# An adaLN transformer pair: order of loads, first offsets, bias pair and third group at the head of layer 0

## The chip, the cores and the metric

The kernel runs on one core of a Trainium2 chip, as one program. The metric is the device time of one execution in microseconds; lower is better. Three executions of the kernel before are given, and one more was taken with a profile.

## The reference

Two adaLN layers over x of shape (4, 1024, 128), float32. The whole change lies in the attention of layer 0:

```python
mod = (_silu(L0_c) @ L0_wmod).reshape(L0_c.shape[0], 6, 1, -1)
sa, ca, ga, sb, cb, gb = (mod[:, i] for i in range(6))
ga = (2 * (ga >= 0) - 1) * jnp.maximum(jnp.abs(ga), 0.25)
h = _layernorm(x) * (1 + ca) + sa
# attention: linear, with a rotary-like product
qkvu = h @ Wqkvu.T + bqkvu              # q, k, v, u; 16 heads of 8
q, k = silu(q), silu(k)
q, k = [t * cos(theta * n), t * sin(theta * n)] for t in (q, k)
out = einsum(q, k) @ v                  # no softmax, so q (k^T v)
out = u * layernorm(out, ln_w, ln_b)
x = x + ga * (out @ Wout.T + bout)
# then: layernorm, modulation, top-2 routing to 8 experts with capacity,
# and a second layer (cosformer attention, 16 routed experts)
```

## The kernel before

Layer 0 works in eight groups of four token tiles (a group is 512 tokens, `G4 = 4`, `NGRP = 8`); two groups are one batch. All engines have a hand-written program each, and they meet only at semaphores. An engine works strictly in the order of its list, so the order of the calls is the schedule.

**Loads.** `l0_sync` (line 188 on) issues all loads from SyncE's queue, one behind the other: the first quarter of the first batch's x (line 196), theta (197), `consts` (198: identity, masks, ones, 713 columns), modulation's weights `wmod` (199, 768 columns), the early rows with the bias of keys and values (200), layer 0's projection weights (201), the second quarter of x (202), then the rest. ScalarE's queue loads `cols`, the per-partition columns.

**Head of each engine's list.** VectorE (`l0_vector`, line 952) takes mean and variance of group 0 (`keys_stats(0)`, helper `variances`, lines 797 to 802), builds the rotation angles for half of the positions (`angles_vector(0)`, lines 760 to 769), takes the statistics of group 1, builds the bias pair (line 790, the key bias split in a high and a low part), closes the angles (lines 776 to 784), builds the other half, and then rotates keys (line 818) and queries (line 845) as they come. `keys_stats(2)` stands behind the first query rotation. GpSimd (`l0_gpsimd`) turns variances into inverse roots and offsets: `keys_roots(u)` gives the negated mean (line 233), the root (line 228) and their product (line 236), the offset that ScalarE adds. It then makes the gate columns (lines 243 to 249), the gated bias `gbo` (line 259), the gated output weights (line 267), and later it sends each tile's rows to the experts' buffer with two indirect DMAs a tile (line 291).

ScalarE (`l0_scalar`) normalises a group (`keys_normed`, line 622: scale and offset), evicts the transposed group with the modulation on it (`keys_modulated`, line 631), makes silu of the keys (line 638), keeps the values (line 644), u and the queries (lines 659, 662), the angles' sines (lines 605, 607) and the transposed rotation tables (`rotation_kept`, line 613). TensorE (`l0_tensor`) makes the modulation (`mod_tensor`, line 348), transposes a group (`keys_turned`, line 385), projects keys (lines 395, 399) and values (line 408), adds up the state k^T v over a batch (`keys_state`, line 436), projects u (line 416) and q (line 422), and multiplies the rotated queries with the state (`outputs_tensor`, line 448).

**The loop.** When groups 0 and 1 have given the first state, a loop over g from 0 to 5 handles output group g, key group g + 2 and input group g - 1 together. In it ScalarE squares the outputs (line 668) for their variance, VectorE gates them (`outputs_gated`, line 854), rotates keys g + 2 (line 818), reads the variances (line 860), rotates the queries of g + 1 (line 845), adds to x (lines 869, 876, 885), takes statistics (line 797) and routes (lines 905 to 950). The input's transposes, bias matmuls and rows are lines 491, 469 and 504 of TensorE. `S["l0_root1"]` counts three increments for each unit of `keys_roots`.

After layer 0's last dispatch the experts' matmuls start from the dispatched rows, and layer 1 follows.

Of the kernel before, what the change touches and what calls it, by code (L numbers as in the profile page):

```python
# [75 lines left out]
class Kernel:  # L76
# [113 lines left out]
    def l0_sync(self):  # L190
        sp, S, io = self.sp, self.S, self.io
# [4 lines left out]
        sp.dma_start(X(0)[:, 0:G4, :], x(0)[:, 0:G4, :]).then_inc(S["dma_x0"], 16)  # L196
        sp.dma_start(self.rowsb[:, 0:D], row(0, D)).then_inc(S["dma_cols"], 16)
        sp.dma_start(self.consts[:], io["consts"]).then_inc(S["dma_consts"], 16)
        sp.dma_start(self.wmod[0][:], io["wmod0"]).then_inc(S["dma_wmod0"], 16)
        sp.dma_start(self.rowsb[:, D:early], row(D, early)).then_inc(S["dma_rows"], 16)  # L200
# [28 lines left out]

    def keys_roots(self, u):  # L230
        g, S, at = self.pool, self.S, self.UNITS[u]
        g.wait_ge(S["ln1"], u + 1)
        g.tensor_scalar(self.nm1[:, at], self.mv1[:, at, 0], -1.0, None, ALU.mult).then_inc(S["l0_root1"], 1)
        self.inverse_root(self.y1[:, at], self.t1[:, at]).then_inc(S["l0_root1"], 1)
        g.wait_ge(S["l0_root1"], 3 * u + 2)
        g.tensor_tensor(self.nm1[:, at], self.nm1[:, at], self.y1[:, at], ALU.mult).then_inc(S["l0_root1"], 1)
# [115 lines left out]
    def gate_tensor(self, lay):  # L352

        pe, S, bank = self.pe, self.S, self.bank
        pe.wait_ge(S["mod_wide"], lay + 1)
        pe.wait_ge(S["dma_consts"], 16)
        if lay:
            pe.wait_ge(S["l0_x"], NGRP)
        for j in range(2):
            for b in range(B):  # L360
                ins = pe.matmul(bank[6 + j][:, b * D:(b + 1) * D], self.gateB[:, j, b, :], self.c["ident"], start=True,
                                stop=True)
            ins.then_inc(S["mod_B"], 1)
# [15 lines left out]
    def keys_turned(self, a):  # L379
        pe, S, bank = self.pe, self.S, self.bank  # L380
        pe.wait_ge(S["l0_xn"], a + 1)
        pe.wait_ge(S["l0_hT"], a)
        pe.wait_ge(S["l0_h2T"], max(0, a - 3))
        for i in range(G4):
            ins = pe.transpose(bank[0][:, i * P:(i + 1) * P], self.xn[:, i, :], self.c["ident"])
# [136 lines left out]
    def l0_tensor(self):  # L522
# [16 lines left out]
        for g in range(NGRP - 2):  # L539
            a, c = g + 2, g - 1  # L540
            self.keys_turned(a)
            self.outputs_tensor(g)
            self.keys_projected(a)
            self.values_projected(a)
# [151 lines left out]
    def l0_scalar(self):  # L696
# [19 lines left out]
        self.rotation_sines(1)  # L716
        self.queries_kept(1)
        self.rotation_kept(1)
        self.keys_normed(2)
        for g in range(NGRP - 2):  # L720
            a, c = g + 2, g - 1
            self.keys_modulated(a)
            self.outputs_squared(g)
            self.keys_silu(a)
            if c >= 0:
# [27 lines left out]
    def angles_vector(self, half):  # L753
# [9 lines left out]
        v.wait_ge(vs.sem, k)  # L763
        k = vs.did(v.tensor_scalar(cnt[:], th[:], 1.0 / TWO_PI, ROUND, ALU.mult, ALU.add))
        v.wait_ge(vs.sem, k)
        k = vs.did(v.tensor_scalar(cnt[:], cnt[:], ROUND, None, ALU.subtract))
# [37 lines left out]
    def keys_stats(self, u):  # L804
# [3 lines left out]
        tiles = [self.X[:, n, :] for n in range(at.start, at.stop)]  # L808
        self.variances(tiles, self.kst1[:, 0:len(tiles), :], self.mv1[:, at, :], self.t1[:, at]).then_inc(S["ln1"], 1)

    def keys_rotated(self, a):
# [140 lines left out]
    def l0_vector(self):  # L952
        v = self.dve
        v.memset(self.label[:], 0.0)
        self.keys_stats(0)
        self.angles_vector(0)
        self.keys_stats(1)
        self.bias_pair()
        self.angles_closed(0)
        self.angles_vector(1)  # L960
        self.keys_rotated(0)
        self.angles_closed(1)
        self.queries_rotated(0)
        self.keys_stats(2)
        self.keys_rotated(1)
# [1664 lines left out]
```

## Time and profile before

| | |
|---|---|
| three executions | 876.41, 876.96, 877.82 us; median 876.96 |
| profiled execution, its own time | 876.81 us |
| its span, first to last instruction | 875.5 us |
| TensorE matmul busy | 813.9 us (93%) |
| VectorE busy | 610.6 us (70%) |
| ScalarE busy | 434.1 us (50%) |
| GpSimd busy | 399.7 us (46%) |
| mean granted clock of TensorE | 0.969 of full |

The span is what the views of the trace cover; the execution's own time is 1.3 us longer. Busy times overlap, so they don't add up to the span. Matmuls are pipelined, so TensorE's busy share is not its share of peak. The chain of waits is followed back from the last instruction to what released each step.

### The profile page before, as it was taken

Reading aid. Unit: us, or ns where it says so; the run is one execution under the profiler, and the core shown is the slowest. Engines: PE = TensorE matmul, PEld = TensorE weight load, DVE = VectorE, ACT = ScalarE, POOL = GpSimd, SP = SyncE. Lnnn points to the kernel's source line nnn. Section 1 sums busy time; section 2 is a strip of 40 time slices with the busy share of each in tenths; the row PEclk is TensorE's granted clock in tenths of the full one; section 3 lists DMA queues with packets and bytes.
Section 4 is the critical chain, followed back from the end, with each engine's and each line's share of the span. In section 5 each row is a group of like instructions: output and inputs, shape, how many; then the busy total and the mean of one; then the engine's idle time right before and its main releaser. Section 6 shows DMA issues by size and latency. Waiting matters only on the chain.

```text
span 875.5 us, 32569 instructions
## 1 busy us (share of the span) xinstructions
PE 813.9 (93%) x13678; PEld 702.7 (80%) x13678; DVE 610.6 (70%) x1760; ACT 434.1 (50%) x947; POOL 399.7 (46%) x404
## 2 busy tenths in 40 slices
PE   6999985399997799999999999999999999999998
PEld 5777755389996688888888888888888888878887
DVE  7788894475663676675677685786866777758875
ACT  5556532443443756555556465464564564433222
POOL 5348887324454554644545654456442342410000
PEclk9999995599998999999999999999999999999999
DMA  9714100434232100000100100200000000027761
GB/s 297 246 52 169 35 29 11 130 121 119 84 93 72 45 27 4 28 3 3 50 4 3 29 3 3 53 3 3 4 3 3 5 3 3 4 52 147 153 134 40
DMA packets 67904, 49.66 MB, mean 57 GB/s; under 512 B 5297, under 2 KB 62784, under 8 KB 67376
## 3 DMA queue, kind: packets, MB, share of 16 engines
q1 hardware_dynamic: 64288, 42.41, 18.0%
q0 software_dynamic: 3328, 5.16, 1.8%
q8 instruction: 109, 1.79, 0.9%
q14 instruction: 35, 0.29, 0.1%
q10 hardware_dynamic: 144, 0.02, 0.0%
HBM read 33.20 MB, written 16.10 MB: 56 GB/s over the span
## 4 chain that ended last, share of the span: by engine, by line
PE 76%; DVE 7%; issue 6%; POOL 5%; ACT 3%; DMA 1%; SPq 0%; ACTq 0%; POOLq 0%; DVEq 0%
PE psum L1477 11%; PE psum L1580 8%; PE psum L1607 7%; PE psum L1558 7%; PE psum L1165 6%; PE psum L2224 5%; PE psum L1510 5%; PE psum L1539 5%; PE psum L2242 4%; PE psum L1595 3%; PE psum L1521 3%; POOL disp L291 3%; PE psum L1495 3%; PE psum L1200 3%; POOL sb_l_y L228 1%
## 5 line engine op out<-in xcount | busy, mean ns | idle before, releaser
L2122 POOL TENSOR_TENSOR sb_a_qr<-sb_h,sb_a_csq 128x512 f32<-128x512 f32 x64 | 81.5, 1296 | 113.8 <-PE psum L1580 107.9
L2122 POOL TENSOR_TENSOR sb_a_qr<-sb_a_qp,sb_a_csq 128x512 f32<-128x512 f32 (+1 forms) x64 | 72.3, 1152 | 116.8 <-PE psum L1580 116.8
L1477 PE MATMUL psum<-sb_wkv,sb_a_hs 128*128 128x512 f32 x384 | 122.2, 427 | 1.9 <-DVE sb_a_hs L1931 1.6
L1734 ACT ACTIVATE sb_a_vr<-sb_a_va,sb_consts 128x520 f32<-128x520 f32 x128 | 86.6, 727 | 5.1 <-DVE sb_a_va L1982 4.7
L291 POOL DMA_INDIRECT disp<-sb_h,sb_slot x64 | 68.7, 1073 | 25.9 <-issue 16.1
L1477 PEld LDWEIGHTS psum<-sb_wkv,sb_a_hs 128*128 128x128 f32 x384 | 63.8, 191 | 13.6 <-DVE sb_a_hs L1931 2.0
L1580 PE MATMUL psum<-sb_a_vr,sb_a_kb 64*64 64x130 f32 x1920 | 73.0, 277 | 1.9 <-issue 1.9
L2003 DVE TENSOR_TENSOR sb_a_mid<-psum,sb_a_state 128x130 f32<-128x130 f32 x112 | 47.4, 424 | 36.6 <-PE psum L1580 36.5
L1111 POOL DMA_INDIRECT chosen<-sb_m_h3t,sb_e_row x40 | 39.4, 985 | 69.3 <-ACTq L1279 53.7
L1558 PE MATMUL psum<-sb_a_mid,sb_a_qr 64*64 64x65 f32 x2048 | 70.6, 218 | 0.0
L1165 PE MATMUL psum<-sb_e_xt,sb_e_ws 128*128 128x320 f32 x384 | 63.8, 321 | 4.5 <-DVE sb_e_hs L1359 3.7
L1711 ACT ACTIVATE sb_h<-psum,sb_cols 128x512 f32<-128x512 f32 x32 | 22.0, 688 | 90.8 <-PE psum L1510 90.8
L1607 PE MATMUL psum<-sb_a_wo,sb_a_ot 128*128 128x128 f32 x512 | 65.5, 281 | 0.0
L1580 PEld LDWEIGHTS psum<-sb_a_vr,sb_a_kb 64*64 64x64 f32 x1920 | 56.9, 132 | 10.3 <-issue 4.9
L1558 PEld LDWEIGHTS psum<-sb_a_mid,sb_a_qr 64*64 64x64 f32 x2048 | 65.1, 134 | 0.0
L1165 PEld LDWEIGHTS psum<-sb_e_xt,sb_e_ws 128*128 128x128 f32 x384 | 58.1, 193 | 8.2 <-issue 5.1
L1558 PE MATMUL psum<-sb_a_state,sb_a_qr 64*64 64x65 f32 x1792 | 62.8, 218 | 0.0
L2224 PE MATMUL psum<-sb_m_hs,sb_wgus 128*128 128x512 f32 x240 | 60.9, 401 | 0.7 <-DVE sb_m_hs L2357 0.7
L1607 PEld LDWEIGHTS psum<-sb_a_wo,sb_a_ot 128*128 128x128 f32 x512 | 59.6, 192 | 1.7
L2300 ACT ACTIVATE sb_m_sg<-psum 128x512 f32<-128x512 f32 x40 | 23.9, 599 | 70.9 <-PE psum L2224 70.9
L1558 PEld LDWEIGHTS psum<-sb_a_state,sb_a_qr 64*64 64x64 f32 x1792 | 58.0, 134 | 0.0
L1982 DVE TENSOR_TENSOR sb_a_va<-psum,sb_rows 128x512 f32<-128x512 f32 x64 | 44.0, 688 | 15.8 <-PE psum L1477 15.8
(276 smaller groups left out, 1946.8 us busy)
## 6 DMA issues: line engine op xcount, KB each, us to landing
sb_h<-turned SPq DMA_DIRECT2D x32, 256.0 KB, 5.5
sb_e_w<-in_w SPq DMA_DIRECT2D x24, 256.0 KB, 3.2
chosen<-sb_empty SPq DMA_DIRECT2D x8, 512.0 KB, 6.5
sb_a_g<-chosen SPq DMA_DIRECT2D x12, 256.0 KB, 3.5
disp<-sb_empty SPq DMA_DIRECT2D x4, 650.0 KB, 9.8
sb_e_x<-disp SPq DMA_DIRECT2D x7, 325.0 KB, 5.2
sb_a_wo<-in_wo SPq DMA_DIRECT2D x4, 512.0 KB, 5.2
out<-sb_x SPq DMA_DIRECT2D x7, 256.0 KB, 3.9
```

Of the source, the lines that this page charges most:

```text
L291: g.indirect_dma_start(out=self.disp, out_offset=bass.IndirectOffsetOnAxis(ap=self.slot[:, k, n:n + 1], axis=0), in_=self.H2[:, n, :], in_ ...
L1165: ins = pe.matmul(bank[2 * (n % 2) + w][:, 0:HC], self.ews[:, i, wp, w, m * P:(m + 1) * P], self.xeT[:, i, xp, cols], start=(k == 0), stop ...
L1477: ins = pe.matmul(self.values_bank(i) if kv else self.bank[0], hs[:, part, at:at + P], self.Wkv[ws][:, h, w], start=(k == 0), stop=(k == 2))
L1510: ins = pe.matmul(self.bank[2], self.Wq[ws][:, j // PH, (j % PH) * P:(j % PH + 1) * P], hs[:, part, :], start=(k == 0), stop=(k == 2))
L1558: ins = pe.matmul(self.bank[4 + q][c * DH:(c + 1) * DH, j * 65:(j + 1) * 65], Qr[p, k, j, r * DH:(r + 1) * DH], states[r][p, j, k, :], sta ...
L1580: ins = pe.matmul(self.bank[bk][q * DH:(q + 1) * DH, at:at + 130], Kb[t, 2 * j + q, :], Vr[t, 2 * j + q, :, :].rearrange("p k d -> p (k d) ...
L1607: ins = pe.matmul(self.bank[1][:, 0:D], self.oT1[:, m, :], self.Wog[b % 2][:, m, :], start=(m == 0), stop=(m == HD // P - 1))
L1734: ins = act.activation(self.Vr[i % 2][:, :, k, :], self.Va[i % 3][:], ACT.Copy, scale=self.c[("cos1", "sin1")[k]][:, n:n + 1])
L1982: v.tensor_tensor(self.Va[i % 3][:, :, 0:DH], self.values_bank(i).rearrange("p (h d) -> p h d", d=DH), self.c["bv1"][:, h * 512:(h + 1) * ...
L2003: ins = v.tensor_tensor(part(mid), first, part(state), ALU.add)
L2122: ins = g.tensor_tensor(self.Qr[i % 2][:, k, :, t], qp, rows(self.csQ[:, k, c * P + t.start:(c + 1) * P], PH), ALU.mult)
L2224: ins = pe.matmul(self.hidden_bank(t, w), self.Wgus[wp][:, w, blk * P:(blk + 1) * P], hs[:, xp, :], start=(n == 0), stop=(n == 2))
```

## The change

It exchanges two loads on SyncE's queue, moves TensorE's wait for the constants from the gate matmuls to the first transpose, gives the first group's offsets to VectorE (one instruction, -mean times root, put into `angles_vector(0)` before its third group of instructions; GpSimd keeps the root alone), puts VectorE's bias pair ahead of the second statistics and its third statistics ahead of the first query rotation, lets ScalarE normalise the third group before it copies the second half of the rotation tables, and in the loop's first turn puts TensorE's key projection before the outputs and ScalarE's silu of the keys before the square.

```diff
         sp.dma_start(self.rowsb[:, 0:D], row(0, D)).then_inc(S["dma_cols"], 16)
+        sp.dma_start(self.wmod[0][:], io["wmod0"]).then_inc(S["dma_wmod0"], 16)
         sp.dma_start(self.consts[:], io["consts"]).then_inc(S["dma_consts"], 16)
-        sp.dma_start(self.wmod[0][:], io["wmod0"]).then_inc(S["dma_wmod0"], 16)
...
     def keys_roots(self, u):
+
         g, S, at = self.pool, self.S, self.UNITS[u]
         g.wait_ge(S["ln1"], u + 1)
+        if u == 0:
+            self.inverse_root(self.y1[:, at], self.t1[:, at]).then_inc(S["l0_root1"], 1)
+            return
...
         pe.wait_ge(S["mod_wide"], lay + 1)
-        pe.wait_ge(S["dma_consts"], 16)
...
         pe.wait_ge(S["l0_h2T"], max(0, a - 3))
+        if a == 0:
+            pe.wait_ge(S["dma_consts"], 16)
...
             self.keys_turned(a)
-            self.outputs_tensor(g)
-            self.keys_projected(a)
+            if g == 0:
+                self.keys_projected(a)
+                self.outputs_tensor(g)
+            else:
+                self.outputs_tensor(g)
+                self.keys_projected(a)
...
         self.queries_kept(1)
+        self.keys_normed(2)
         self.rotation_kept(1)
-        self.keys_normed(2)
         for g in range(NGRP - 2):
             a, c = g + 2, g - 1
             self.keys_modulated(a)
-            self.outputs_squared(g)
-            self.keys_silu(a)
+            if g == 0:
+                self.keys_silu(a)
+                self.outputs_squared(g)
+            else:
+                self.outputs_squared(g)
+                self.keys_silu(a)
...
         k = vs.did(v.tensor_scalar(cnt[:], th[:], 1.0 / TWO_PI, ROUND, ALU.mult, ALU.add))
+        if half == 0:
+            self.first_keys_offsets()
         v.wait_ge(vs.sem, k)
...
+    def first_keys_offsets(self):
+        v, S, at = self.dve, self.S, self.UNITS[0]
+        v.wait_ge(S["l0_root1"], 1)
+        v.scalar_tensor_tensor(self.nm1[:, at], self.mv1[:, at, 0], -1.0, self.y1[:, at], ALU.mult, ALU.mult
+                               ).then_inc(S["l0_root1"], 2)
...
         self.angles_vector(0)
+        self.bias_pair()
         self.keys_stats(1)
-        self.bias_pair()
         self.angles_closed(0)
         self.angles_vector(1)
         self.keys_rotated(0)
         self.angles_closed(1)
+        self.keys_stats(2)
         self.queries_rotated(0)
-        self.keys_stats(2)
         self.keys_rotated(1)
```

## Rows read from the trace of the kernel before

**Rows 1.** Chain of waits: start us, us, what
```profile
34.29 1.10 PE psum L399 x8
...
60.90 1.22 POOL disp L291
```

**Rows 2.** Windows: us, busy (x instructions) by engine, PEclk, DMA share, GB/s
```profile
51.00:52.00 1.00, 1.00 (x7) 1.00 (x7) 0.55 (x1) 0.85 (x2) 1.00 (x3) 0.50 0.00 0
...
60.00:80.00 20.00, 19.30 (x132) 15.22 (x131) 16.56 (x69) 11.94 (x24) 15.79 (x14) 1.00 0.64 225
```

**Rows 3.** VectorE's timeline: start, us, line, tiles, [idle before <-releaser]
```profile
6.58 0.43 DVE L766 TENSOR_SCALAR sb_cnt<-sb_cnt 128x512 f32<-128x512 f32 x1
...
10.00 0.87 DVE L797 BATCH_NORM_STATS2 sb_l_st<-sb_x 128x6 f32<-128x128 f32 x4 [0.79 <-DMA sb_x<-in_x]
...
11.40 0.33 DVE L790 SCALAR_TENSOR_TENSOR sb_l_pair<-sb_l_high,sb_cols,sb_rows 2x128 fp32r<-2x128 f32 x1
...
13.79 0.69 DVE L784 SCALAR_TENSOR_TENSOR sb_tokt<-sb_tokt 128x512 f32<-128x512 f32 x1
...
18.68 2.40 DVE L818 TENSOR_TENSOR sb_kr<-sb_ks,sb_tokt 128x512 f32<-128x512 f32 x2
...
23.71 1.29 DVE L845 TENSOR_TENSOR sb_qr<-sb_q_t,sb_dimt 128x512 f32<-128x512 f32 x2
24.91 0.87 DVE L797 BATCH_NORM_STATS2 sb_l_st<-sb_x 128x6 f32<-128x128 f32 x4
...
36.04 1.30 DVE L818 TENSOR_TENSOR sb_kr<-sb_ks,sb_tokt 128x512 f32<-128x512 f32 x2 [0.77 <-ACT sb_ks L638]
```

**Rows 4.** GpSimd's timeline
```profile
5.48 0.30 POOL L233 TENSOR_SCALAR sb_l_nm<-sb_l_mv 128x4 f32<-128x4 f32 x1 [3.54 <-DVE sb_l_t L802]
5.75 1.30 POOL L228 TENSOR_TENSOR sb_l_y<-sb_l_t,sb_cols 128x4 f32<-128x4 f32 x1
7.12 0.67 POOL L236 TENSOR_TENSOR sb_l_nm<-sb_l_nm,sb_l_y 128x4 f32<-128x4 f32 x1
...
12.75 1.44 POOL L228 TENSOR_TENSOR sb_l_y<-sb_l_t,sb_cols 128x4 f32<-128x4 f32 x1
...
26.49 0.62 POOL L233 TENSOR_SCALAR sb_l_nm<-sb_l_mv 128x4 f32<-128x4 f32 x1 [5.96 <-DVE sb_l_t L802]
...
28.61 0.20 POOL L236 TENSOR_TENSOR sb_l_nm<-sb_l_nm,sb_l_y 128x4 f32<-128x4 f32 x1
```

**Rows 5.** ScalarE's timeline
```profile
27.73 1.06 ACT L613 COPY sb_dimt<-psum 128x512 f32<-128x512 f32 x2
28.84 1.65 ACT L622 ACTIVATE sb_xn<-sb_x,sb_l_nm,sb_l_y 128x128 f32<-128x128 f32 x4
31.24 0.78 ACT L631 ACTIVATE sb_h_t<-psum,sb_mt 128x512 f32<-128x512 f32 x1 [0.75 <-PE psum L385]
```

**Rows 6.** SyncE's queue: start and length of the issue of the constants
```profile
1.78 0.42 SPq L198 DMA_DIRECT2D sb_consts<-in_consts  x1
```

**Rows 7.** DMA issues: count, KB each, median us from issue to landing
```profile
sb_consts<-in_consts SPq DMA_DIRECT2D x1, 356.5 KB, 5.0
```

**Rows 8.** TensorE's timeline
```profile
7.81 2.73 PE L348 MATMUL psum<-sb_sc,sb_wmod 128*128 128x4 f32 x12 [7.81 <-DMA sb_wmod<-in_wmod]
...
27.81 1.96 PE L436 MATMUL psum<-sb_v,sb_kr 128*128 128x129 f32 x16
...
31.90 1.96 PE L448 MATMUL psum<-sb_qr,sb_kvc 128*128 128x512 f32 x4 [0.70 <-issue]
```

**Rows 9.** Chain of waits in two turns of the loop, at half and full clock
```profile
50.20 0.91 PE psum L491 x4
...
52.82 1.52 PE psum L504 x8
...
65.67 0.66 PE psum L491 x4
...
67.21 1.18 PE psum L504 x8
```

## The prediction, made before the changed kernel ran

> **What bounds the kernel now.** I read the chain of waits first, then the windows by stage, then each engine's timeline from 0 to 60 us. In the chain the third group's key projection holds 34.29 to 35.39 us, and the first dispatch of tokens to the experts' buffer is at 60.90 [rows 1]; the experts start behind the last dispatch. Whatever reaches the first dispatch earlier can pass to the end, because from there GpSimd is the paced engine: 15.79 of 20 us busy from 60 to 80 us, the rest being the gaps between its dispatches [rows 2]. So the question is how much earlier VectorE starts the third group's key rotation, its 36.04 us row [rows 3]; behind that row its timeline runs without a gap into the statistics that release GpSimd's next roots.
>
> In the front itself VectorE sets the pace: it waits 0.79 us for the second quarter of x, starts at 10.00, and its rows then follow each other without idle time up to the statistics of the third group at 24.91 [rows 3]. Those release GpSimd's three root instructions at 26.49, which end at 28.61 + 0.20 = 28.81 [rows 4]; ScalarE normalises at 28.84 and modulates at 31.24 [rows 5].
>
> **The change, part by part.**
> 1. *wmod before constants.* Same two issues, same bytes behind them; only their places at 1.78 us and the next slot are exchanged. The constants landed 5.0 us after issue, at 6.8 [rows 6, 7]; wmod was waited for until 7.81 [rows 8]. I take wmod at 6.9 and constants at 7.75 (their sizes differ by a tenth). TensorE starts its modulation 0.9 earlier. Constants are wanted by ScalarE's bias copies, by GpSimd's copies and now by the first transpose; all come after 7.75, so nothing is queued for long behind the moved wait.
> 2. *First offsets by VectorE.* GpSimd dropped two instructions: 0.30 before the root, 0.67 behind it. The root (1.30) now starts at 5.48 and ends at 6.78 [rows 4]. VectorE stops ahead of its second count instruction, which started at 6.58 [rows 3], until 6.82, adds one small instruction, and goes on about 0.35 later. The nearest row to that instruction is the bias pair, the same operation on 128 columns: 0.33, with the next one starting 0.26 behind it [rows 3]. On 4 columns I take 0.1; bounds 0 and 0.26, so the delay is 0.25 to 0.5. Cover: the 0.79 wait for x. Without that cover it would cost 0.35. Normalising starts near 7.0 in place of 7.83.
> 3. *Bias pair before the second statistics.* It took the path from 11.40 to 11.66 [rows 3]. Now it needs ScalarE's high part: normalising from 7.0, 1.65 long as at 28.84 [rows 5], then two short copies, about 9.1. VectorE arrives at 10.00 - 0.79 + 0.35 = 9.55, finishes by 9.85, inside the same wait for x. Gain on the VectorE path **0.26**; if ScalarE is late by over 0.8, the gain goes.
> 4. *Results for ScalarE and GpSimd at the head.* First modulated tile, gate columns, second normalising are all about 0.9 earlier. Nothing of this ends on the path: the angles on VectorE gate the first key rotation. Only ScalarE's query step of the second group gains: between 0 and 0.9, I take 0.35, as TensorE's unchanged projections stand between. The gate-times-bias product on GpSimd (128x512) comes 0.9 earlier too. In the trace the first rotation took 2.40 against 1.29 for the same shape in the query rotation [rows 3], 1.1 of it beside that product. I leave the 1.1 unchanged: the product now meets the last angle instruction and then the rotation; bounds 0 (all of it hidden, gain 1.1) and a second blocked instruction (loss 0.7).
> 5. *Third statistics before the first query rotation.* Query rotation started at 23.71, statistics at 24.91: 1.20 sooner, plus the 0.26. GpSimd starts at 26.49 - 1.46 = 25.03. Its three instructions took 2.32 (26.49 to 28.81). Now they run wholly beside VectorE's two-input instructions. At 7.12, beside VectorE's angle instructions, the last of the three took 0.67, not 0.20 [rows 4], so 2.32 to 2.8: offsets ready at 27.35 to 27.8, I take **27.7** against 28.81. The query rotation moves by its own length to 24.9 and the second key rotation still ends at its old time less 0.26, as the order changes but not the sum.
> 6. *ScalarE normalises before copying the rotation.* The copies started 27.73 and took 1.06; the normalising was at 28.84 and took 1.65 [rows 5]. ScalarE is free at about 27.4, so: normalise 27.7 to 29.35, copies to 30.35, modulate (0.78) to 31.1; before, 31.24 + 0.78 = 32.02. TensorE's state matmuls end at 27.81 + 1.96 - 0.22 = 29.55 [rows 8], the transposes follow at once, ready by 30.2, before ScalarE wants them.
> 7. *Key projection before outputs, silu before square.* Projection (1.1 for its last matmuls [rows 1]) ends at about 32.3, silu at 33.0; before, silu came behind the outputs. Outputs started at 31.90 [rows 8], directly behind the second state. That comes 0.22 sooner, but they now wait for the projection: 32.2, which costs **+0.3**. Its square and the gated product move with it; the product ended at 36.04 - 0.77 = 35.27, now at 35.55. The keys are ready by then, so the 0.77 that VectorE waited for them [rows 3] is gone. Key rotation starts at 35.5 in place of 36.04.
>
> **Sum.** -0.77 (wait for keys) + 0.3 (outputs behind projection), so **-0.47 us** at 36.04, and with step 5 at its short end (27.35, projection 0.2 sooner) about -0.65. All that follows (variance, roots of group 3 and 4, statistics) is released by VectorE or by GpSimd behind VectorE; the variance matmuls had been done before VectorE came to them. I carry the middle, -0.55, to the end. The profiled execution took 876.81 (span 875.5), 0.15 under the median of the runs, 876.96; taking the median: 876.96 - 0.55 = **876.4**.
>
> **A rule that speaks against it.** In the trace a root (12.75, 1.44) had VectorE's angle instruction, both inputs in SBUF, start inside it at 13.79 and take its usual 0.69 [rows 3, 4]: a small GpSimd instruction did not hold VectorE off. The Trainium skill, "SBUF — State Buffer", Who interferes with whom, says that of a VectorE instruction with two SBUF inputs and a GpSimd instruction that reads SBUF the later one is blocked until the first is through. By that rule the third root, now placed among two rotations, would stop VectorE for up to its 1.44, and the time would lie between the forecast and rival C; the 2.40 row agrees with the rule, the 0.69 row [rows 3] does not.
>
> **Rivals.**
> - *A, less than it says.* wmod lands no sooner (both transfers share the same engines), or the sum is lost at another engine, for example ScalarE's copies holding the modulation. Without step 1, ScalarE is free at 27.75, modulation at 31.2 becomes 31.4, and -0.55 shrinks to -0.3: **876.7**. For: the two landings lie only 1 us apart. Against: the constants did land a full microsecond sooner than wmod.
> - *B, the clock.* TensorE's granted clock is half (1.2 GHz) from 51 to 52 us [rows 2], behind short gaps in its work. That iteration's matmuls up to the routing ended 52.82 + 1.52 = 54.34, counted from the transposes at 50.20 that is 4.14; one iteration later at the full 2.4 GHz the same stretch is 65.67 to 68.40, 2.73 (its last piece 1.18) [rows 9]. It is on the path. If the changed timing spares it, another 1.4: 876.4 - 1.4 = **875.0**. For: only a short fall, so little may avoid it. Against: the gaps stay.
> - *C, slower: GpSimd holds VectorE.* If each of the three instructions of step 5 gets in front of a rotation and keeps it off, VectorE loses 0.25 + 1.45 + 0.20 = 1.9 between 25 and 29 us. The second key rotation, the state and the outputs go with it: outputs at 33.5 to 35.4, key rotation of group three at 36.75, 0.7 later than before: **877.7**. It decides once over 1.2 us of blocking falls before the second key rotation ends. Against: the 13.79 row [rows 3].
> - *D, the clock the other way.* A further half-clock stretch on the path, the same 1.4 [rows 9] on top: **877.8**. TensorE has fewer gaps from 29 to 36 than before, which speaks against.
>
> **How the numbers follow.** 0.2% is 1.75 us, about what a measurement of this kernel can tell from no change. The forecast, 876.4, has 0.58; A 0.12, B 0.20, C 0.05, D 0.05. Faster by over 0.2% is under 875.2: most of B and a small part of the forecast (product of step 4 wholly hidden, -1.1 more): 0.24. Slower is over 878.7: C or D with another loss on top, 0.05. Same 0.71. The range takes in B and the small ends of C and D: 874.8 to 877.7.
>
> **What the changed profile would show.** wmod's matmuls near 6.9; normalising of the first group near 7.0; no bias pair between the second statistics (still 10.0) and the angles; angles 0.26 sooner; GpSimd's third root from 25.0; normalising 27.7; outputs' matmuls 32.2, behind the projection; key rotation at 35.5 without a wait for ScalarE's keys; first dispatch at 60.3; last dispatch landing 0.55 sooner. Wrong if: x's second quarter lands later than 10.0; VectorE stands longer at the first offsets than 0.79; the second key rotation takes over 1.3; or the first dispatch moves and the end does not.

## The result and the profile after

| | median of the kernel before | median after | ratio, 95% interval |
|---|---|---|---|
| eight executions each, one chip | 877.32 us | **874.40 us** | 0.9967 [0.9957, 0.9977] |

The change makes the kernel 2.9 us (0.33%) faster; the interval leaves out both the forecast of 0.55 us and no change. The forecast of 876.4 us and its whole range, 874.8 to 877.7, missed the median. The profiled execution took 874.18 us (span 872.9), against 876.81 (875.5).

Landmarks in the two profiles, in us from the start of the span. Start of VectorE's rows unless another engine is named:

| | before | after | difference |
|---|---|---|---|
| second statistics (x's second quarter has landed) | 10.00 | 10.34 | +0.34 |
| third statistics | 24.91 | 23.75 | -1.16 |
| ScalarE's third normalising | 28.84 | 27.77 | -1.07 |
| TensorE's first outputs | 31.90 | 32.09 | +0.19 |
| key rotation of group 3 | 36.04 | 35.30 | -0.74 |
| TensorE's first input transposes | 50.20 | 49.46 | -0.74 |
| first dispatch on GpSimd | 60.90 | 58.75 | -2.15 |
| span | 875.5 | 872.9 | -2.6 |

Two things stand out. The key rotation came 0.74 sooner although x had landed 0.34 later, so the part in between became **1.08 us** shorter: twice the forecast. And between transposes and first dispatch another 1.41 us went. A last 0.45 of the span's 2.6 went behind the first dispatch; it was not traced.

VectorE's timeline after (start, us, line, tiles, idle before and its releaser), the rows that answer to [rows 3]:

```profile
6.74 0.16 DVE L829 SCALAR_TENSOR_TENSOR sb_l_nm<-sb_l_mv,sb_l_y 128x4 f32<-128x4 f32 x1 [0.16 <-POOL sb_l_y L228]
...
9.57 0.34 DVE L805 SCALAR_TENSOR_TENSOR sb_l_pair<-sb_l_high,sb_cols,sb_rows 2x128 fp32r<-2x128 f32 x1
10.34 0.87 DVE L812 BATCH_NORM_STATS2 sb_l_st<-sb_x 128x6 f32<-128x128 f32 x4 [0.42 <-DMA sb_x<-in_x]
...
18.84 2.27 DVE L839 TENSOR_TENSOR sb_kr<-sb_ks,sb_tokt 128x512 f32<-128x512 f32 x2
...
34.70 0.69 DVE L875 TENSOR_TENSOR sb_ou<-psum,sb_u_t 128x512 f32<-128x512 f32 x1 [1.44 <-ACT sb_sq L677]
35.30 1.28 DVE L839 TENSOR_TENSOR sb_kr<-sb_ks,sb_tokt 128x512 f32<-128x512 f32 x2
```

The first offsets wait 0.16 for GpSimd's root and take 0.16; the bias pair lies wholly inside what was a 0.79 wait for x and is now 0.42. The first key rotation still takes 2.27. VectorE no longer waits for the keys ahead of the last row; its wait is now 1.44 for the square, ahead of gating the outputs.

ScalarE's timeline after, answering to [rows 5]:

```profile
6.94 1.65 ACT L631 ACTIVATE sb_xn<-sb_x,sb_l_nm,sb_l_y 128x128 f32<-128x128 f32 x4 [1.61 <-DVE sb_l_nm L829]
...
18.92 0.69 ACT L668 ACTIVATE sb_u_t<-psum,sb_cols 128x512 f32<-128x512 f32 x1 [0.27 <-PE psum L421]
...
27.77 1.65 ACT L631 ACTIVATE sb_xn<-sb_x,sb_l_nm,sb_l_y 128x128 f32<-128x128 f32 x4
29.32 1.04 ACT L622 COPY sb_dimt<-psum 128x512 f32<-128x512 f32 x2
30.27 0.78 ACT L640 ACTIVATE sb_h_t<-psum,sb_mt 128x512 f32<-128x512 f32 x1
```

GpSimd's, answering to [rows 4]: the first root alone, the wait for the later constants, and the third group's offsets.

```profile
5.50 1.13 POOL L228 TENSOR_TENSOR sb_l_y<-sb_l_t,sb_cols 128x4 f32<-128x4 f32 x1 [3.55 <-DVE sb_l_t L817]
7.78 0.29 POOL L309 COPY sb_h<-sb_consts 128x32 f32<-128x32 f32 x1 [1.15 <-DMA sb_consts<-in_consts]
...
27.44 0.29 POOL L240 TENSOR_TENSOR sb_l_nm<-sb_l_nm,sb_l_y 128x4 f32<-128x4 f32 x1
```

TensorE's, answering to [rows 8] and the full- and half-clock rows of [rows 9]: modulation, the gate matmuls (L364), outputs, input transposes and rows.

```profile
6.80 2.51 PE L352 MATMUL psum<-sb_sc,sb_wmod 128*128 128x4 f32 x11 [6.80 <-DMA sb_wmod<-in_wmod]
...
14.93 3.09 PE L364 MATMUL psum<-sb_consts,sb_gateb 128*128 128x128 f32 x16
...
32.09 1.88 PE L453 MATMUL psum<-sb_qr,sb_kvc 128*128 128x512 f32 x4
...
49.46 0.66 PE L496 MATMUL psum<-sb_consts,sb_xn 128*128 128x128 f32 x4 [0.81 <-ACT sb_xn L684]
...
50.98 1.19 PE L509 MATMUL psum<-sb_consts,sb_h_t 128*128 128x136 f32 x8
```

The chain of waits after: from the square on it is VectorE's again, and the first dispatch stands at its end. It answers to [rows 1].

```profile
31.10 1.16 PE psum L404 x8
32.26 1.73 PE psum L453 x4
34.01 0.61 ACT sb_sq L677
...
58.75 1.22 POOL disp L295
```

The windows after, against the half clock in [rows 2]:

```profile
50.00:51.00 1.00, 1.00 (x11) 0.83 (x9) 0.81 (x2) 0.85 (x2) 1.00 (x3) 1.00 0.00 0
51.00:52.00 1.00, 1.00 (x9) 1.00 (x9) 0.69 (x1) 1.00 (x4) 1.00 (x1) 1.00 0.00 0
```

The granted clock is 1.00 (2.4 GHz) where the profile of before had 0.50 (1.2 GHz). From the transposes to the router's scores on VectorE it was 4.17 us before and is 2.75 after: that is the 1.41. So the change seems to have done rival B on top of twice the forecast. The experiments show that only the latter is the change's.

### The profile page after: what moved, and what is told of

It is laid out like the page before. It is cut to its first block, busy times and chain, and to the rows that moved or that the text cites. A ratio compares the mean times of both kernels' runs of the same rounds, so it can differ in the third digit from the quotient of the medians.

```text
span 872.9 us, 32569 instructions
## 1 busy us (share of the span) xinstructions
PE 813.6 (93%) x13678; PEld 702.2 (80%) x13678; DVE 610.7 (70%) x1761; ACT 433.8 (50%) x947; POOL 397.8 (46%) x402
## 4 chain that ended last, share of the span: by engine, by line
PE 76%; DVE 7%; issue 6%; POOL 5%; ACT 3%; DMA 1%; SPq 0%; ACTq 0%; POOLq 0%; DVEq 0%
PE psum L1498 11%; PE psum L1601 8%; PE psum L1628 7%; PE psum L1579 7%; PE psum L1186 6%; PE psum L2245 5%; PE psum L1531 5%; PE psum L1560 5%; PE psum L2263 4%; PE psum L1542 3%; PE psum L1616 3%; POOL disp L295 3%; PE psum L1516 3%; PE psum L1221 3%; POOL sb_l_y L228 1%
```

## The experiments

I write **S** for the stretch from the second statistics to group 3's key rotation (26.04 before, 24.96 after). It takes out when x lands. The chips of the experiments take about 10 us longer for either kernel; part of it lies behind the head (in the whole change's profiles the experts' part, up to layer 1's first projection, took 118 to 122 us for 114). All times are medians, compared with the kernel before on the same chip; 12 or 11 executions each unless one is named.

**The parts, and a filler for the clock.** The third group alone:

```diff
+        self.keys_normed(2)
         self.rotation_kept(1)
-        self.keys_normed(2)
...
+        self.keys_stats(2)
         self.queries_rotated(0)
-        self.keys_stats(2)
```

and with it keys_projected(a) and keys_silu(a) first in the turn g == 0, as in the change.

> Only the third group's part: third statistics before the first query rotation, normalising before the rotation copies, and in the loop's first turn keys before outputs. Theory T1 (the order of the third group makes the shift, and the half-clock stretch at 50.7 us of the profiled run of before goes by chance of its phase): key rotation of group 3 at 35.7 against 36.04 (the bias pair's 0.26 is not saved), first dispatch 0.35 us sooner where the half-clock stretch is still there and 1.75 sooner where not; median 0.5 to 2 us under before. Theory T2 (the half-clock stretch goes because TensorE's work from 29 to 47 us lies otherwise; it is this part that moves it): the stretch is gone in nearly all runs, so about 1.8 to 2.2 us under before. Theory T3 (the head, not the third group, carries the gain): under 0.3 us.

Measured: 888.34 us against 889.60, ratio 0.9995 [0.9977, 1.0012]; S 25.59.

The head alone: exchanged loads, moved wait, first offsets, bias pair; the rest as before.

> Only the head: wmod before the constants, first offsets by VectorE, bias pair before the second statistics. T1: 0.2 to 0.3 us sooner at the key rotation of group 3 (the bias pair's 0.26), the half-clock stretch as often as in before: median 0.2 to 0.6 under before. T2: half-clock stretch stays, 0.25 under before. T3: more than half of the 2.9 us of the whole change.

Measured: 888.73, ratio 0.9990 [0.9969, 1.0010]; S 25.71.

The kernel before with eight idle matmuls into an unused bank, so that TensorE's gaps ahead of the input transposes are filled:

```diff
             self.squares_summed(g)
+            if g == 1:
+                pe, bank = self.pe, self.bank
+                pe.wait_ge(self.S["l0_x"], 1)
+                for i in range(2):
+                    pe.matmul(bank[7][:, 0:P], self.c["ident"], self.c["ident"], start=True, stop=True)
             self.normed_output(g)
+            if g == 1:
+                for i in range(6):
+                    pe.matmul(bank[7][:, 0:P], self.c["ident"], self.c["ident"], start=True, stop=True)
             if g:
                 self.input_turned(c)
```

> The kernel before with 8 matmuls more, in the gaps of TensorE at 47.9 and 49.4 us, into a PSUM bank that is free there; they are no part of the computation. If the half-clock stretch at 50.7 comes from these gaps and lies on the path: no half clock between 50 and 55, the stretch from the input's transposes to the routing 2.8 in place of 4.1, the kernel about 1.4 us under before (1.0 to 1.6, where the fillers hold the transposes up by up to 0.2). If the stretch is rare in runs of before: no difference. If its cause lies earlier: it stays.

Measured: 889.96, ratio 1.0011 [0.9994, 1.0029]; full clock at the transposes (2.71 us from them to the scores), S 26.04. The transposes themselves stood 0.36 later behind the second statistics (40.56 for 40.20), so the scores came 1.10 sooner. The whole change with the same filler:

> The whole change with the same 8 matmuls. T1 and T2: the half-clock stretch is already gone in most runs, so the same as the changed kernel within 0.4 us, 2.4 to 3.2 under before. If phases decide (T1) and some runs of the changed kernel still have it, a little faster than the changed kernel.

Measured: 887.73, ratio 0.9989 [0.9974, 1.0004]; S 24.96.

What follows: the parts gave -0.45 and -0.33 of S, the whole -1.08, so 0.30 came only with both. The table further down shows where: in the third group alone ScalarE started the normalising 0.34 behind its offsets. The filler brought the full clock in its profile and no time in the median, which would have had to fall by about 1.1 us if the kernel before usually had the half clock there; the interval allows 0.5.

**The unchanged kernel again, and the whole, on a second chip**, with two that leave a part out of the whole. Leaving out the third group's sooner norm:

```diff
+        self.rotation_kept(1)
         self.keys_normed(2)
-        self.rotation_kept(1)
...
+        self.queries_rotated(0)
         self.keys_stats(2)
-        self.queries_rotated(0)
```

Leaving out the sooner keys:

```diff
-            if g == 0:
-                self.keys_projected(a)
-                self.outputs_tensor(g)
-            else:
-                self.outputs_tensor(g)
-                self.keys_projected(a)
+            self.outputs_tensor(g)
+            self.keys_projected(a)
...
-            if g == 0:
-                self.keys_silu(a)
-                self.outputs_squared(g)
-            else:
-                self.outputs_squared(g)
-                self.keys_silu(a)
+            self.outputs_squared(g)
+            self.keys_silu(a)
```

> The kernel before, run as if it were a changed one: what difference two equal programs show on this chip, and whether the half-clock stretch at 50 us is there in another of its profiles. All theories: no difference, ratio within 0.1% of 1. T1 (the stretch is a matter of phase): it may be absent at 50 us. T2 (it is a fixture of the old order): it is there.

> The whole change again, in the same batch. Counted from the start of the second statistics (the landing of x's second quarter) its third key rotation comes 1.08 us sooner than in before, as in the first pair of profiles. T1: the runs' medians differ by 1.0 to 1.6 us, and the 2.9 of the first comparison is not reached again unless this chip's runs of before spend more windows at half clock. T2: 2.5 to 3 us.

> The whole change without the third statistics and the third normalising moved ahead; the loop's first turn still has keys before outputs. T1: the modulated third group comes no earlier than in before less 0.26, so keys first holds the outputs back until about 33.2, and the key rotation of group 3, counted from the second statistics, is later than with the whole change by 1.0 or more: no gain left or a loss to 0.3 against before. Rival (keys first pays by itself): it keeps over half of the 1.08.

> The whole change with outputs before keys in the first turn, as before. T1: the outputs start with the state, 0.26 to 0.33 sooner, but keys and silu stay behind them, so the key rotation of group 3 gains those 0.3 only: 25.7 us behind the second statistics, against 26.04 in before and 24.96 with the whole change. Rival (the early normalising pays by itself): 25.3 or less.

Measured: unchanged 889.22 (ratio 0.9982 [0.9956, 1.0008], which shows how much of 0.2% chance leaves); whole 887.79, 0.9972 [0.9946, 0.9998]; no sooner norm 889.18 and no sooner keys 889.25, one execution each.

The whole's windows here:

```profile
49.00:50.00 1.00, 0.94 (x5) 0.94 (x6) 1.00 (x3) 0.48 (x2) 1.00 (x1) 0.50 0.00 0
50.00:51.00 1.00, 1.00 (x6) 1.00 (x6) 0.41 (x1) 0.79 (x2) 1.00 (x3) 0.50 0.00 0
```

The half clock at the transposes (49.06 here) is back with the whole change, S being 24.95, and it is absent from the unchanged kernel's profile. In all 20 profiles it falls on this place in 6: the kernel before's first, the whole's here and in a later run, and those of three other versions. The mean granted clock of the timed executions agrees: in the three later comparisons of the whole it was 0.969 for both, over 35 executions of the whole and 85 of the kernel before. **Whether the half clock falls there is chance in either kernel; the 1.41 us of the first pair is not the change's.**

S was 25.71 without the sooner keys, just the head's, although the third normalising stood 1.11 us sooner than in the head (17.43 us behind the second statistics for 18.54). So in the old order the normalising doesn't set S. The chain of waits of this version passes through the second state and VectorE's closing of it (`sb_kvc`) to the outputs:

```profile
28.11 2.07 PE psum L440 x16
...
31.78 0.44 DVE sb_kvc L847
32.22 0.09 issue
32.31 1.96 PE psum L452 x4
```

The sooner norm needs the sooner keys to count. Without the sooner norm S was 27.66, but with the half clock at the outputs (33 to 36 us; 3.52 us for them, 1.96 in [rows 8]), so I took it again below.

The unchanged kernel gave the surprise: **S 27.04 in place of 26.04**. Its TensorE, ScalarE and second key rotation:

```profile
16.65 3.08 PE L361 MATMUL psum<-sb_consts,sb_gateb 128*128 128x128 f32 x16
...
20.63 0.69 ACT L659 ACTIVATE sb_u_t<-psum,sb_cols 128x512 f32<-128x512 f32 x1 [0.28 <-PE psum L416]
...
27.06 1.29 DVE L818 TENSOR_TENSOR sb_kr<-sb_ks,sb_tokt 128x512 f32<-128x512 f32 x2
...
28.51 1.04 PE L376 MATMUL psum<-sb_consts,sb_tokt 128*128 128x128 f32 x8
...
29.38 1.96 PE L436 MATMUL psum<-sb_v,sb_kr 128*128 128x129 f32 x16
...
30.23 1.65 ACT L622 ACTIVATE sb_xn<-sb_x,sb_l_nm,sb_l_y 128x128 f32<-128x128 f32 x4
```

against the first profile of the same kernel:

```profile
16.08 2.08 PE L361 MATMUL psum<-sb_consts,sb_gateb 128*128 128x128 f32 x16
...
19.16 0.69 ACT L659 ACTIVATE sb_u_t<-psum,sb_cols 128x512 f32<-128x512 f32 x1
...
26.34 1.30 DVE L818 TENSOR_TENSOR sb_kr<-sb_ks,sb_tokt 128x512 f32<-128x512 f32 x2
...
26.94 1.04 PE L376 MATMUL psum<-sb_consts,sb_tokt 128*128 128x128 f32 x8
...
31.38 0.42 DVE L835 SCALAR_TENSOR_TENSOR sb_kvc<-sb_kvs,sb_kvm 128x256 f32<-128x256 f32 x1
```

TensorE's first matmuls take about twice as long as the same ones later (L399 x8 2.08 at 12.51 us, 1.16 once the group comes round again), until some point between 15 and 19 us. The clock column prints 1.00 there in every profile, so I go by durations; "the clock rises" in the expectations means this point. Here it fell behind the 16 gate matmuls, which took 3.08. ScalarE waited for them and its u came 1.47 later. So did what follows in TensorE's and ScalarE's lists: the transposes of the second half of the rotation tables (L376) and, 0.87 behind them, the second state (L436), 1.57 later than in the first profile, though its key rotation was through at 28.35; and the third normalising, 1.4 later and long after its offsets (ready at 28.92). x itself had landed 0.57 later.

**Once more, for the spread.** Whole and unchanged again, no sooner norm again, and a version of the whole in which VectorE rotates group 3's keys before it gates the first outputs, in the idle time in front of the square:

```diff
-            self.outputs_gated(g)
-            if c >= 0:
+            if g == 0:
+                self.keys_rotated(a)
+                self.outputs_gated(g)
+            else:
+                self.outputs_gated(g)
                 self.input_means(c)
-            self.keys_rotated(a)
+                self.keys_rotated(a)
```

> The whole change a third time. Key rotation of group 3 starts 24.96 us behind the second statistics (before: 26.04). If the shift of 1.08 us is all that the change does beside chance in the clock's windows, the means over all batches come to 1.0 to 1.4 us under before; if the change also spares half-clock windows as a rule, its runs show about one window fewer each than those of before and a mean of 1.8 to 2.5 us under.

> The kernel before once more as a partner: its mean number of half-clock windows and its time should fall with the runs of before, within 0.1%. It tells how large a difference comes from nothing.

> The whole change without the earlier third statistics and normalising, again, as in the last look a half-clock window fell on its output matmuls (3.52 us for 1.96). At full clock its key rotation of group 3 starts 26.1 us behind the second statistics: keys first gives nothing without the earlier normalising. If 25.7 or less, the two parts are independent.

> The whole change, and VectorE in the loop's first turn rotates the third group's keys before it gates the outputs: with the keys ready 1.4 us before the square, the rotation fits the 1.44 us in which VectorE waits. Theory (the outputs behind the keys are what now holds VectorE): the gating stays at its time, the variance is read at once when it is there, and the next query rotation comes 0.7 to 0.9 us sooner than with the whole change; first dispatch about 0.8 sooner at equal clock. If the chain runs over GpSimd or ScalarE by then: under 0.2.

Measured: whole 884.36 us against 886.26, 0.9984 [0.9969, 0.9999], S 24.96; unchanged 886.15, 1.0009 [0.9992, 1.0026], S 26.90, gate matmuls 2.94; no sooner norm 885.11, one execution, S 25.95, which is 0.24 more than the head's, as the outputs now wait for keys that are no sooner; keys rotated first 885.41, 0.9991 [0.9975, 1.0007]. In that last one the rotation started at 32.84, 2.1 sooner than the whole's, and nothing came of it: the transposes were 39.11 behind the second statistics, as in the whole. Its VectorE, then GpSimd:

```profile
32.84 2.35 DVE L838 TENSOR_TENSOR sb_kr<-sb_ks,sb_tokt 128x512 f32<-128x512 f32 x2
```

```profile
31.64 3.01 POOL L270 TENSOR_TENSOR sb_wog<-sb_wos,sb_gate 128x512 f32<-128x512 f32 x2 [4.23 <-DVE sb_kvc L855]
```

Beside GpSimd's gated output weights the rotation took 2.35 for 1.28, and the weights 3.01 for 2.49.

**What protects the path, and a version beyond.** The whole without the exchange of the two loads; the exchange alone in the kernel before; the whole; and the whole with keys rotated first and the gated output weights freed of a wait that only placed them:

```diff
         g.wait_ge(S["l0_wog"], 2)
-        g.wait_ge(S["l0_kvc"], 1)
```

> The whole change without the exchange of the two loads: wmod behind the constants again, TensorE's wait for the constants back at the gate matmuls; first offsets, bias pair, third group as in the change. Measured from the second statistics (x's second quarter) to group 3's key rotation. Theory L (the load order does it: TensorE starts a microsecond sooner, its clock rises sooner, the third group's modulation matmuls are through before ScalarE needs them): TensorE starts near 7.8 again, and in a profile whose clock rises after 18 us ScalarE stands waiting and the stretch goes from 25.0 to about 26; no wait at ScalarE if the clock rises by 17 us. Theory O (the order of the third group does it, since normalising goes ahead of the copies and has slack): 25.0 whichever way the clock rises. Both: TensorE's modulation near 7.8 in place of 6.9. Time against before: L, -0.5 to -1.0 us; O, -1.7 us.

> The kernel before with the exchange of the two loads and the moved wait for the constants alone. Theory L: the stretch from the second statistics to group 3's key rotation is at most 26.04 (25.7 to 26.04) however late x comes, since the clock rises before 17 us; never 26.9 to 27.0, as two profiles of the unchanged kernel had it with a rise at 18.5 to 19 us. Time against before -0.3 to -0.9 us. Theory O: the stretch is spread like that of the kernel before, 26.04 to 27.0, and the time is before's within 0.3 us. Both: modulation's first matmul at 6.9.

> The whole change, and two more moves: VectorE rotates the keys of group 3 before it gates the first outputs, and GpSimd makes the gated output weights (128x512) without waiting for group 2's keys and values, so that they run at 27.7 to 30.2 us while VectorE has nothing to do and not beside the key rotation, which took 2.35 us in place of 1.28 when it was rotated first beside them. Theory P (two engines holding each other off): key rotation near 32.8 and 1.3 long, the following waits for ScalarE and TensorE short, input's transposes 0.7 to 1.0 sooner behind the second statistics than the whole's 39.1, that is 38.1 to 38.4; time 0.5 to 0.9 us under the whole. Rival: the stretch is paced by TensorE and ScalarE by now (projection, outputs, square), and the transposes stay at 39.1 and the time at the whole's.

> The whole change again, beside the three others on one chip. Both theories: second statistics to group 3's key rotation 24.95, modulation from 6.9, clock rise before 17.5 us, first dispatch 48.4 behind the second statistics (49.8 if a half-clock stretch falls on the input's transposes near 50 us). Time 1.7 us under before; and level with the kernel without the exchange of loads by theory O, 0.7 to 1.2 under it by theory L.

Measured, all against 886.26 us: no exchange 885.39, 0.9983 [0.9966, 0.9999], S 25.38; exchange alone 885.57, 0.9989 [0.9975, 1.0003], S 25.96; gates sooner 884.46, 0.9977 [0.9961, 0.9993]; whole 885.01, 0.9982 [0.9967, 0.9996], S 24.96. The times of the first two don't part from the whole's; the profiles do. Without the exchange S lay between the two theories of its expectation (about 26, and 25.0). ScalarE without the exchange:

```profile
19.49 0.69 ACT L666 ACTIVATE sb_u_t<-psum,sb_cols 128x512 f32<-128x512 f32 x1 [0.28 <-PE psum L419]
...
28.16 1.63 ACT L629 ACTIVATE sb_xn<-sb_x,sb_l_nm,sb_l_y 128x128 f32<-128x128 f32 x4
```

The offsets were ready at 27.75; ScalarE was 0.4 late for them. And gates sooner, VectorE, then GpSimd:

```profile
29.39 0.43 DVE L845 TENSOR_TENSOR sb_kvm<-psum,sb_consts 128x256 f32<-128x256 f32 x1 [2.16 <-PE psum L439]
...
32.70 1.29 DVE L837 TENSOR_TENSOR sb_kr<-sb_ks,sb_tokt 128x512 f32<-128x512 f32 x2
```

```profile
27.24 2.50 POOL L269 TENSOR_TENSOR sb_wog<-sb_wos,sb_gate 128x512 f32<-128x512 f32 x2
```

The weights now fill VectorE's 2.16 us of waiting, the rotation takes its 1.29, and the input transposes stand 38.42 behind the second statistics, 0.69 sooner than the whole's 39.11, as expected. The median is 0.55 us under the whole's, which the intervals can't tell from nothing. It is the version with the shortest path of those tried.

**TensorE made late on purpose.** Modulation's weights one place further behind, in the whole (without its exchange, and with the wait for the constants back at the gate matmuls) and in the kernel before:

```diff
         sp.dma_start(self.consts[:], io["consts"]).then_inc(S["dma_consts"], 16)
+        sp.dma_start(self.rowsb[:, D:early], row(D, early)).then_inc(S["dma_rows"], 16)
         sp.dma_start(self.wmod[0][:], io["wmod0"]).then_inc(S["dma_wmod0"], 16)
-        sp.dma_start(self.rowsb[:, D:early], row(D, early)).then_inc(S["dma_rows"], 16)
```

> The change without its exchange of loads, and modulation's weights put one place further behind (constants, early rows, then wmod), so that TensorE starts near 8.5 us and keeps the doubled matmul durations (16 gate matmuls in about 3 us in place of 2.1) longer. Theory L (only the early load spares the path): ScalarE waits for TensorE near 20 us, the third normalising and group 3's key rotation slip, 26.0 or more from the second statistics to the key rotation. Theory O (the third group's new order has slack of its own): at most 25.4, as in the version without the exchange of loads, although the gate matmuls take 3 us.

> The kernel before with wmod one place further behind in the same way. Both theories: the doubled durations last into the gate matmuls (about 3 us for the 16, in place of 2.08), and the stretch from the second statistics to group 3's key rotation is 26.9 or more, as in the two profiles of the unchanged kernel with slow gate matmuls. If it stays at 26.04 with gate matmuls of 3 us, what those two profiles lost came from elsewhere, and theory L falls.

One execution each: 886.91 and 888.02 against 887.14. TensorE started at 9.55 and 8.89, later than I meant. ScalarE of the late whole and of the late before:

```profile
21.43 0.69 ACT L666 ACTIVATE sb_u_t<-psum,sb_cols 128x512 f32<-128x512 f32 x1
...
30.09 1.63 ACT L629 ACTIVATE sb_xn<-sb_x,sb_l_nm,sb_l_y 128x128 f32<-128x128 f32 x4
```

```profile
20.95 0.70 ACT L659 ACTIVATE sb_u_t<-psum,sb_cols 128x512 f32<-128x512 f32 x1
...
30.46 1.65 ACT L622 ACTIVATE sb_xn<-sb_x,sb_l_nm,sb_l_y 128x128 f32<-128x128 f32 x4
```

S was 26.48 and 27.28. The first contradicts theory O, which had at most 25.4: the new order of the third group has no slack of its own for a late TensorE.

**What S follows in either order.** Both orders hang on ScalarE's first u, and so on the gate matmuls, but at different joins.

In the old order the first outputs wait for VectorE's `sb_kvc`, which closes the second state (in the first profile it ended at 31.80, and the outputs started at 31.90), and the key projection stands behind them. The state's matmuls start at the later of two times: 0.05 behind the end of VectorE's second key rotation, and 0.87 behind the start of TensorE's own transposes of the tables, which come 7.8 to 7.9 us behind the first u. From the state's start to the outputs it is 4.09 to 4.20 us, and from there to the key rotation 4.13 or 4.14, in all eight profiles with outputs first. The third normalising has room there: in the first profile the modulated group was ready at 32.02, and its projection began at 33.79, behind the outputs.

In the new order the key projection stands ahead of the outputs, and in the eight such profiles with the sooner norm (VectorE's order as in the change) 7.53 to 7.56 us lie between the third normalising and S's end. The normalising starts at the later of its offsets and ScalarE's own list, about 8.67 behind the first u (9.5 to 9.6 in the old order, with the copies ahead).

The last six columns count from the second statistics, the others from the start of the span.

| profile | TensorE starts | gate matmuls: start, us | first u | second key rotation ends | tables + 0.87 | state starts | offsets ready | normalising | S |
|---|---|---|---|---|---|---|---|---|---|
| *outputs first* | | | | | | | | | |
| before | 7.81 | 16.08, 2.08 | 19.16 | 17.64 | 17.81 | 17.81 | 18.81 | 18.84 | 26.04 |
| before + filler | 8.00 | 16.50, 2.08 | 19.58 | 17.62 | 17.81 | 17.81 | 18.80 | 18.84 | 26.04 |
| unchanged | 7.85 | 16.65, 3.08 | 20.63 | 17.78 | 18.81 | 18.81 | 18.35 | 19.66 | 27.04 |
| unchanged | 7.78 | 16.42, 2.94 | 20.26 | 17.64 | 18.67 | 18.67 | 18.82 | 19.53 | 26.90 |
| before, late | 8.89 | 17.02, 2.44 | 20.95 | 18.10 | 19.05 | 19.06 | 19.28 | 19.91 | 27.28 |
| exchange alone | 6.88 | 15.98, 1.95 | 18.82 | 17.58 | 17.54 | 17.63 | 18.75 | 18.79 | 25.96 |
| head alone | 6.86 | 14.98, 2.86 | 18.73 | 17.33 | 17.22 | 17.39 | 18.51 | 18.54 | 25.71 |
| whole, no sooner keys | 6.98 | 15.10, 2.36 | 18.88 | 17.33 | 16.79 | 17.38 | 17.39 | 17.43 | 25.71 |
| *keys first* | | | | | | | | | |
| third group alone | 7.84 | 16.58, 2.38 | 19.86 | 17.63 | 18.12 | 18.12 | 17.69 | 18.03 | 25.59 |
| whole, no exchange | 7.80 | 15.93, 2.67 | 19.49 | 17.36 | 17.91 | 17.91 | 17.42 | 17.83 | 25.38 |
| whole, late | 9.55 | 17.67, 2.86 | 21.43 | 17.98 | 19.00 | 19.01 | 18.04 | 18.92 | 26.48 |
| whole, after | 6.80 | 14.93, 3.09 | 18.92 | 17.33 | 17.33 | 17.39 | 17.39 | 17.43 | 24.96 |
| whole, second chip | 6.93 | 14.96, 1.95 | 18.11 | 17.32 | 16.79 | 17.38 | 17.38 | 17.42 | 24.95 |

In the kernel before TensorE's list came last at the state even in its two fast profiles, by 0.17 and 0.19 us. So a late TensorE costs it in full, about 1 us in two of four profiles. The whole starts its gate matmuls 1.0 to 1.9 us sooner: even with the slowest, 3.09 us, the offsets still came last, by 0.14. The exchange alone moves the gate matmuls only to 15.98, since the key projection then waits 1.20 us for the bias pair; the head alone, with both, had 14.98. So exchange and bias pair belong together.

## Why the prediction was wrong

**Right:** steps 1 to 3. wmod's matmuls at 6.80 for 6.9 forecast, constants used from 7.78 (7.75), normalising at 6.94 (7.0), the bias pair inside the wait for x. The first key rotation kept most of the 1.1 us that it lost beside the gate product (2.27 for 1.29). Step 5's 1.46 sooner was 1.50, counted from the second statistics (14.91 us before, 13.41 after). The wait for keys went, as in the sum. Rival C, GpSimd holding VectorE, did not come: the two rotations beside the third root took 1.29 each. Of the signs of being wrong one came true, x's second quarter after 10.0 (10.34); counting from its landing takes that out.

**Mis-sized, in steps 5 to 7.** Counted from the second statistics at 10.00, offsets were ready at 27.39, the short end of 27.35 to 27.8 of which I took 27.7: 0.3. From the normalising to the key rotation it was 7.53 us against my 7.8 (27.7 to 35.5): the outputs did come behind the projection, but at 31.75 and not 32.2. The normalising 0.27 sooner and the rest 0.27 shorter make 0.54, which turns my -0.54 (35.5 for 36.04) into -1.08. In the terms of the sum: the outputs, forecast 0.3 later, came 0.15 sooner (21.90 to 21.75 behind the second statistics), and from them to the key rotation 0.93 went (4.14 to 3.21), where I had 0.77.

**Failed: step 4's "Nothing of this ends on the path: the angles on VectorE gate the first key rotation".** The first key rotation is not where TensorE's early start arrives; the second state is. I followed only VectorE's rotation into it ("In the front itself VectorE sets the pace"), and TensorE's own list, through the gate matmuls and ScalarE's first u, came later already in the one profile that I had: tables' transposes at 26.94, state at 27.81, rotation through at 27.64. That profile showed a fast case. In two other profiles of the same kernel the gate matmuls took 3 us, the state started 1.03 us behind the rotation's end, and the path lost 1.0 and 0.86 us more. The forecast treated the kernel before as one timeline, and counted no gain for making TensorE early. The mean S over the four profiles of the kernel before (one with the filler) is 26.51, over the five of the whole (one with the filler) 24.96: **-1.55 us**, of which 1.08 is the steady part and 0.47 what the slow cases no longer cost. Four profiles don't tell how often the slow case comes.

**Against the times.** Three later comparisons of the whole gave -1.92, -1.90 and -1.25 us (medians; by the ratios -2.5, -1.4 and -1.6), in line with -1.55. The first gave -2.9 [-3.8, -2.0]. The 1.3 us between stays open: the half clock at the transposes, 1.41 us a time, is a candidate, as it fell in that chip's profile of before and not in that of after, but a profile shows one execution. The mean granted clock of after's eight executions there was 0.972, above the 0.969 of either kernel on the other chips; of before's only the profiled one's is on record, 0.969. x's second quarter may also land sooner (10.18 on average in twelve profiles with wmod first, 10.36 in six without; the two late kernels left out; each spreads over nearly 0.6 or more). Neither was settled.

**Rivals.** A (less than it says) was right on one point: without the exchange the gain shrinks, by 0.42 of S, where A had 0.25. B happened in the first pair of profiles and is chance. D, a further half-clock stretch, hit one version at 33 to 36 us, with the same price of about 1.6 us.

## What to carry to other kernels

Before calling an early step free, trace each input of the next joins back, not only the one that seems to come last: two that end within 0.2 us of each other are both the path, and here the one that hung on TensorE's first, slow matmuls moved from run to run. One profile shows one draw of that; a second profile of the unchanged kernel is the cheapest experiment. A quantity that moves together with the path, as the third normalising did in the old order, need not be on it; a version that moves it alone tells. Price a change between two landmarks inside the span, here from a load's landing to a rotation, and ask of any part that a repetition doesn't show whether it was the clock's.

## What the runs showed of the hardware

- TensorE's first matmuls took about twice as long as the same ones later (2.08 us for 1.16) for 8 to 11 us behind its first: the same 16 gate matmuls, starting between 14.6 and 17.7 us, took from 1.95 to 3.09 us. The clock column printed 1.00 there. The Trainium skill, "TensorE: Matmul & The Clock Gate", Part 1, does say that the cold part varies from run to run in the same kernel, and the spread here agrees.
- GpSimd's large instructions held VectorE off: the key rotation took 2.35 for 1.28 us beside the 128x512 product (which took 3.01 for 2.49), and one 128x512 VectorE instruction with a single input took 1.51 for 0.41 beside the gate product in the late kernel. The Trainium skill, "SBUF — State Buffer", Who interferes with whom, has both cases (two SBUF inputs; a tensor_scalar in a 2-port mode, which the trace doesn't show). Beside the 4-column root (1.44 us) rotations took their usual 1.29, which that rule alone would not give.
- The half clock at the input transposes came and went between executions of one kernel, at a price of 1.30 to 1.42 us each time (4.05 to 4.17 us from the transposes to the scores in place of 2.75).
